# Layer-1 experts in half tiles: two 64-token halves of one tile, each with its own expert and weights

## What is computed

```
scores = sigmoid(x @ gate_w.T)
topv, topi = top_k(scores, 2);  topv = topv / topv.sum()
dw[token, topi] += topv
y = shared_mlp(x)
for each expert e:                      # silu(x@w1.T) * (x@w3.T), then @ w2.T
    y += mlp_e(x) * dw[:, e]
```

## Time and profile before

| | us |
|---|---|
| median of 3 runs | 1307.13 |
| lowest and highest | 1302.79, 1315.53 |
| span of the profiled execution, first to last instruction (the page gives no other time for it) | 1301.1 |
| PE busy | 1046.2 |
| DVE busy | 912.1 |
| ACT busy | 491.2 |
| POOL busy | 466.3 |

### The profile page before, as it was taken

The page is one execution under the profiler, slowest core; times in us unless marked ns, Lnnn a source line. Parts: engine busy times, 40 slices in busy tenths (PEclk is TensorE's granted clock), DMA queues, the critical chain, the costliest instruction groups (busy, mean ns, idle before and its releaser), DMA issues.

```text
span 1301.1 us, 18688 instructions
## 1 busy us (share of the span) xinstructions
PE 1046.2 (80%) x6112; PEld 621.6 (48%) x6112; DVE 912.1 (70%) x1502; ACT 491.2 (38%) x1114; POOL 466.3 (36%) x333
## 2 busy tenths in 40 slices
PE   1989898777778788873777778998898979998785
PEld 1644555444444444441634444564455635554343
DVE  3186576889998989896547646666665566756686
ACT  2110035544554544551112134445543454435332
POOL 1000010688888888862180012333232313331000
PEclk9798899989998988895879798999898989989798
DMA  9900071689987888889530043544253525441121
GB/s 360 340 5 0 1 189 41 139 141 155 158 149 132 149 137 152 148 129 180 121 122 4 12 90 77 114 106 103 68 125 79 119 61 128 92 98 34 25 72 51
DMA packets 111187, 143.26 MB, mean 110 GB/s; under 512 B 30022, under 2 KB 97334, under 8 KB 110902
## 3 DMA queue, kind: packets, MB, share of 16 engines
q0 software_dynamic: 34464, 77.92, 33.4%
q1 hardware_dynamic: 76630, 64.14, 17.8%
HBM read 72.80 MB, written 39.46 MB: 86 GB/s over the span
## 4 chain that ended last, share of the span: by engine, by line
PE 28%; DMA 16%; DVE 10%; issue 6%; POOL 4%; ACT 4%; SPq 3%; ACTq 0%; DVEq 0%; POOLq 0%
DMA sum<-yo,to_i 11%; PE bank L1395 4%; PE bank L1402 3%; PE bank L1823 3%; PE bank L1862 3%; DMA crow<-cp_d 2%; PE bank L1806 2%; DVE cv L2051 2%; PE bank L1815 2%; POOL xg L1148 2%; POOL sum L1141 2%; PE bank L666 2%; PE bank L1848 1%; PE bank L678 1%; PE bank L1389 1%
## 5 line engine op out<-in xcount | busy, mean ns | idle before, releaser
L1468 POOL DMA_INDIRECT sum<-yo,to_i x48 | 76.4, 1592 | 319.9 <-ACT yo L1422 299.8
L1148 POOL DMA_INDIRECT xg<-xn_d,token_i x80 | 99.7, 1247 | 243.6 <-DVE to_i L441 160.4
L1141 POOL DMA_INDIRECT sum<-yo,to_i x80 | 160.8, 2010 | 45.5 <-issue 44.6
L988 PE MATMUL bank<-areaA,xgT 128*128 x320 | 130.8, 537 | 16.4 <-issue 12.8
L1005 PE MATMUL bank<-areaA,hidT 88*128 x320 | 92.7, 414 | 42.7 <-ACT hidT L1053 32.4
L1993 DVE TENSOR_TENSOR areaD<-areaD,gb 128x512 f32<-128x512 f32 x128 | 87.3, 687 | 24.2 <-ACT areaD L1949 23.2
L1949 ACT ACTIVATE areaD<-bank 128x512 f32<-128x512 f32 x128 | 75.9, 594 | 62.7 <-PE bank L1815 59.7
L1121 DVE TENSOR_TENSOR_SCAN xnT<-areaB,xnT 128x1024 f32<-128x1024 f32 x42 | 96.2, 2290 | 3.3
L1005 PEld LDWEIGHTS bank<-areaA,hidT 88*128 88x128 f32 x320 | 56.9, 197 | 76.0 <-issue 71.1
L988 PEld LDWEIGHTS bank<-areaA,xgT 128*128 128x128 f32 x320 | 61.1, 209 | 61.7 <-issue 46.6
L666 PE MATMUL bank<-xnT,areaB 128*128 128x512 f32 x192 | 89.2, 613 | 0.8 <-DVE y L696 0.8
(11 more groups left out here) (327 smaller groups left out, 2210.3 us busy)
## 6 DMA issues: line engine op xcount, KB each, us to landing
y<-xnT POOLq DMA_DIRECT2D x21, 1024.0 KB, 8.9
wst<-gu_f SPq DMA_DIRECT2D x96, 176.0 KB
y<-areaB POOLq DMA_DIRECT2D x11, 1024.0 KB, 8.6
wst<-down_f SPq DMA_DIRECT2D x48, 176.0 KB
gu_f<-in_gu POOLq DMA_DIRECT2D x1, 5632.0 KB, 19.8
areaA<-in_gu SPq DMA_DIRECT2D x2, 2816.0 KB
sum<-yo SPq DMA_DIRECT2D x2, 2176.0 KB, 18.0
down_f<-in_down POOLq DMA_DIRECT2D x1, 2816.0 KB, 25.9
```

Source lines behind the costliest of these rows:

```text
L988: last = nc.tensor.matmul(bank[:, GB + q % 2, 0:2 * FI], xgT[:, q % 2, k, :], wgu0_of(e, k), start=(k == 0), stop=(k == KD - 1))
L1141: nc.gpsimd.indirect_dma_start(sum0_d[q % 2], bass.IndirectOffsetOnAxis(ap=to_i[:, q:q + 1], axis=0), yo[:, q % 5, :], None, compute_op=AL ...
L1148: nc.gpsimd.indirect_dma_start(xg[:, q % 5, :], None, xn_d[0], bass.IndirectOffsetOnAxis(ap=token_i[:, q:q + 1], axis=0)).then_inc(s.gathe ...
L1468: nc.gpsimd.indirect_dma_start(sum1_d, bass.IndirectOffsetOnAxis(ap=to_i[:, q:q + 1], axis=0), yo[:, q % 4, :], None, compute_op=ALU.add). ...
```

## The change

Layer 1's tiles keep 128 rows, but each is now two units of 64 rows with an expert of its own. Experts are padded to multiples of 64, so that 40 tiles (80 units) hold the worst case. `UNITS = (1, 2)` says so for the two layers; the two spare columns (`AHEAD`) of the routing tables fall away in both. For each half, gate, up and down use that half's weights: every product of 128 token columns becomes two of 64 columns, which write partitions 0 to 63 and 64 to 127 of the same bank. SP reads two expert numbers and loads two sets of weights per tile, one transfer for each expert's gate and up and one for its down. Gate and up get two slots (`wgu1`), reloaded after the gate and up product of tile q-2; down gets three (`wd1`), reloaded as before. ACT reads two expert numbers and copies the routing weights in two halves. Functions that nothing called (`route_tensor`, `route_vector`, `shared_tensor`, `shared_scalar`, `shared_vector`) are deleted, so line numbers fall by up to 180.

```diff
-def tiles_of(k):
-    n = (T * k + E * (P - 1)) // P
+HALF = P // 2
+UNITS = (1, 2)
+def tiles_of(k, units):
+    rows = P // units
+    n = -(-((T * k + E * (rows - 1)) // rows) // units)
     return n + n % 2
...
-        vec.done(nc.vector.tensor_tensor(m["cmp"], incl[:, :, TT - 1:TT].to_broadcast([P, E, E]),
-                                         iota128[:, None, :].to_broadcast([P, E, E]), ALU.is_gt))
+        vec.done(nc.vector.tensor_tensor(m["cmp"], incl[:, :, TT - 1:TT].to_broadcast([P, E, E * UNITS[l]]),
+                                         iota64[:, None, ::2 // UNITS[l]].to_broadcast([P, E, E * UNITS[l]]), ALU.is_gt))
...
+        NU = (NT0, NT1)[l] * UNITS[l]
+        vec.done(nc.vector.tensor_tensor(m["q_cmp"], m["tile_end"].unsqueeze(1).to_broadcast([P, NU, E]),
+                                         iota[:, 0:NU, None].to_broadcast([P, NU, E]), ALU.is_le))
...
+    HALVES = [slice(i * HALF, (i + 1) * HALF) for i in range(2)]
+    def experts_of(eng, q):
+        return [eng.value_load(expert_i[0:1, 2 * q + i:2 * q + i + 1], min_val=0, max_val=E - 1) for i in range(2)]
...
             if part == 2 and 1 <= q <= NT1:
                 eb = EB + (q - 1) % 2
+                pe.wait_ge(wd_in[(q - 1) % WR], 32 * ((q - 1) // WR + 1))
                 pe.wait_ge(q1.hT_ready, q)
                 for h in range(2):
-                    last = nc.tensor.matmul(bank[:, eb, 0:D], hidT[:, (q - 1) % 2, h, :], wd_of(q - 1, h), start=(h == 0), stop=(h == 1))
+                    for i, r in enumerate(HALVES):
+                        last = nc.tensor.matmul(bank[r, eb, 0:D], hidT[:, (q - 1) % 2, h, r], wd_of(q - 1, i, h), start=(h == 0), stop=(h == 1))
                 last.then_inc(q1.y_full, 1)
             if part == 2 and q < NT1:
                 eb = EB + q % 2
-                pe.wait_ge(w_in_slot[q % WR], 16 * (3 * (q // WR) + 3))
+                pe.wait_ge(wgu_in[q % WG], 32 * (q // WG + 1))
                 pe.wait_ge(q1.xT_ready, q + 1)
                 for k in range(KD):
-                    last = nc.tensor.matmul(bank[:, eb, 0:2 * FI], xgT[:, q % 2, k, :], wgu_of(q, k), start=(k == 0), stop=(k == KD - 1))
+                    for i, r in enumerate(HALVES):
+                        last = nc.tensor.matmul(bank[r, eb, 0:2 * FI], xgT[:, q % 2, k, r], wgu_of(q, i, k), start=(k == 0), stop=(k == KD - 1))
                 last.then_inc(q1.gu_full, 1)
...
-                e = act.value_load(expert_i[0:1, q:q + 1], min_val=0, max_val=E - 1)
+                e = experts_of(act, q)
                 act.wait_ge(q1.xT_full, q + 1)
-                nc.scalar.activation(slot_w[:, q % 4:q % 4 + 1], xg[:, q % 4, bass.ds(D + e, 1)], ACT.Copy)
+                for i, r in enumerate(HALVES):
+                    nc.scalar.activation(slot_w[r, q % 4:q % 4 + 1], xg[r, q % 4, bass.ds(D + e[i], 1)], ACT.Copy)
...
-                e = sp.value_load(expert_i[0:1, q:q + 1], min_val=0, max_val=E - 1)
+                e = experts_of(sp, q)
+                if q >= WG:
+                    sp.wait_ge(q1.gu_full, q - WG + 1)
+                for i in range(2):
+                    sp.dma_start(wgu1[:, q % WG, i, :].rearrange("p (k f) -> p k f", k=KD),
+                                 gu1_f[bass.ds(e[i], 1), :, :].rearrange("e (k p) f -> p (e k) f", k=KD)).then_inc(wgu_in[q % WG], 16)
                 if q >= WR:
                     sp.wait_ge(q1.y_full, q - WR + 1)
-                for k in range(KD):
-                    sp.dma_start(wgu_of(q, k), gu1_f[bass.ds(e, 1), k * P:(k + 1) * P, :].rearrange("e p f -> (e p) f")).then_inc(w_in_slot[q % WR], 16)
-                sp.dma_start(wst[0:FH, q % WR, KD * 2 * FI:].rearrange("p (h d) -> p h d", h=2),
-                             down1_f[bass.ds(e, 1), :, :].rearrange("e (h f) d -> f (e h) d", h=2)).then_inc(w_in_slot[q % WR], 16)
+                for i in range(2):
+                    sp.dma_start(wd1[:, q % WR, i, :].rearrange("p (h d) -> p h d", h=2),
+                                 down1_f[bass.ds(e[i], 1), :, :].rearrange("e (h f) d -> f (e h) d", h=2)).then_inc(wd_in[q % WR], 16)
```

More of the change, by code:

```diff
@@ L243, in combine_store @@
         sp.dma_start(xn_d[l].rearrange("(t p) d -> p t d", p=P)[:, :, D:], m["combine"]).then_inc(ly[l].xn_stored, 16)
-    def route_tensor(pe, l, K, wr, nr, m):
-        s = ly[l]
-        NT = (NT0, NT1)[l] + AHEAD
-        pe.wait_ge(s.tr_free, KD * TT // 4)
-        pe.wait_ge(s.w_router, 16 * (2 - l))
-        for t in range(TT):
-            for k in range(KD):
-                last = nc.tensor.matmul(bank[:, 4, t * nr:(t + 1) * nr], xnT[:, k, t * P:(t + 1) * P], wr[:, k, :],
-                                        start=(k == 0), stop=(k == KD - 1))
-        last.then_inc(s.logits, 1)
-        pe.wait_ge(s.mask_ready, l + 1)
-        nc.tensor.matmul(bank[:, 5, 0:TT * E], before[:, :], m["mask"], start=True, stop=True).then_inc(s.ranks, 1)
-        nc.tensor.matmul(bank[:, 6, 0:TT * E], ones[:, :], m["mask"], start=True, stop=True).then_inc(s.ranks, 1)
-        pe.wait_ge(s.onehots, l + 1)
-        for n in range(TT * K):
-            last = nc.tensor.matmul(bank[:, 7, 0:NT], m["row_1h"][:, n, :], m["tile_1h"][:, n, :],
-                                    start=(n == 0), stop=(n == TT * K - 1))
-        last.then_inc(s.tokens, 1)
     def side_bank(pe, free, n):
@@ L291, in route_tokens_tensor @@
         s = ly[l]
[L292 removed]
+        NT = (NT0, NT1)[l]
         pe.wait_ge(s.onehots, l + 1)
@@ L543, in route_memory @@
+        nc.vector.scalar_tensor_tensor(to_i[:, 0:NT], m["q_sum"][:, 0:NT], -1.0, bank[:, 6, 0:NT], ALU.add, ALU.add).then_inc(s.indices, 1)
     def route_memory(scr, l, K, nr):
-        NT = (NT0, NT1)[l] + AHEAD
+        NT = (NT0, NT1)[l]
         at = [0]
@@ L606, in shared_scalar @@
-    def shared_scalar(act, l, F, th, beside=None):
-        s = ly[l]
-        def block(c):
-            for f in range(F):
-                act.wait_ge(s.sh_in, c * F + f + 1)
-                act.wait_ge(s.sh_free, c * F + f + 1)
-                nc.scalar.activation(th[:, f % 2, :], bank[:, 2 * (f % 2), :], ACT.Tanh, scale=0.5).then_inc(s.sh_tanh, 1)
-        if beside is None:
-            with act.Fori(0, NB) as c:
-                block(c)
-        else:
-            for c in range(NB):
-                block(c)
-                beside(c)
@@ L1217, in _program @@
     PAIRS = CH // 2
-    WF, WR = KD * 2 * FI + 2 * D, 3
+    WG, WR = 2, 3
     with ExitStack() as c1a, ExitStack() as c1:
@@ L1309, in _program @@
         ring_free = [sem(f"ring_free{k}") for k in range(2)]
-        w_in_slot = [sem(f"w_in_slot{k}") for k in range(WR)]
+        wgu_in = [sem(f"wgu_in{k}") for k in range(WG)]
+        wd_in = [sem(f"wd_in{k}") for k in range(WR)]
         ST, XT, CS, YB, EB = 2, 5, 3, 4, 6
```

194 lines of the change are left out of this document (22 added, 172 removed).

## The result

| | before | after |
|---|---|---|
| median, us | 1308.27 (1302.79 to 1315.53, 4 runs) | 1363.11 (1354.73 to 1366.43, 4 runs) |
| profiled span, us | 1301.1 | 1360.9 |
| mean granted clock of the span | 0.908 | 0.879 |

The change is slower: 1.037 of the time before, 95% interval 1.033 to 1.041. The two medians of the table stand 54.8 us (4.2%) apart, so the loss is 48 to 55 us. I had forecast 1312 with a range up to 1332, so the result lies outside, behind even rival B's 1341.

The account below looks back on a forecast made before the run. PE was taken to set the pace in steps with experts, ACT and DVE in projections. Span 1301.1 - 22.0 + 2.4 + 18.2 + 4 + 2 + 1 = 1306.7, plus 6.0 gives 1312.7, stated as 1312 us; range 1289 to 1332.

Parts of the forecast that it names:

- rival B: SP's queue: pieces back up behind doubled weights, 4 us instead of 2.1 on 11 chunks, more half clock: 1341 us; chance 0.26.
- +18.2 us forecast: SP's queue: total cost of small pieces arriving later behind the weights, over 11 chunks near weights and 4 others.
- +4 forecast: PE's clock: one or two more half-clock stretches after long waits, less one in the part without experts; bounds 0 to 10.
- 2.1 us per chunk: SP's queue: delay of pieces that follow weights: moved wait +1.0, four transfers for three +0.4, doubled bytes ahead +0.7.
- The slack: Chunks' pieces: of 11 near weights, six had no slack, three a little (1.4 us each), two enough; four others 0.3 each.
- the upper bound of 32: SP's queue: top of the 11 to 32 us range for late pieces, by the bounds of issue and queue.
- -22.0: Batches 2 and 3: saving from eight tiles fewer: steps 8.4, to step 8's transposes 4.9, convolutions 4.5, gates 4.2 us.
- covered in the steps: ACT: an extra copy and number read, some 0.5 us per tile, hidden by idle time in steps; +2 overall, bounds 0 to 7.
- I forecast 8.7: Projections of batch 3: saving without experts, from convolutions 4.5 us and gates 4.2 us.
- rival C: PE: the halves run one after the other instead of side by side, adding 90 us: 1403 us; chance 0.02.
- my 0 to 6: PE: bounds on the halves' cost from one more grouping change per tile; taken as 0.06 us a tile, 2.4 us.
- Over 40 us is B: Sign in PE's waits for pieces: about 27 us forecast, under 15 the faster rival (0.24), over 40 the slower queue-backup rival.

Follow-up runs that it names:

- e3: Kernel before, with SP's weights also waiting for the gate and up product of tile q-2; bytes, transfers and tiles unchanged: 1335.85 us, 1.0234.
- e8: Changed kernel, own transfer order, with 16 identity products on PE in front of each chunk's wait for its pieces while experts run: 1364.83 us, 1.0419.
- e13: Changed kernel, own transfer order, with 7 identity products on PE in front of each chunk's wait for its pieces: 1358.0 us, 1.0346.
- e9: Changed kernel, weights of a step's first three ticks behind the pieces, expert numbers and routing-weight copies on POOL instead of ACT: 1287.92 us, 0.9892.
- e11: Kernel before, small pieces ahead of the weights, its one expert number and copy on POOL instead of ACT: 1285.08 us, 0.9842.
- e10: Changed kernel in its own transfer order, expert numbers and routing-weight copies on POOL instead of ACT: 1360.4 us, 1.0443.
- e12: Kernel before, small pieces ahead of the weights, ACT reading the number twice and copying routing weights in two halves: 1298.12 us, 0.9966.
- e6: Changed kernel, weights of a step's first three ticks behind the pieces, ACT's number reads and routing copies behind its gathered rows' copy: 1308.52 us, 0.9975.
- e2: Kernel before, with SP issuing a chunk's small pieces ahead of the weights: 1287.82 us, 0.9874.
- e7: Kernel before, small pieces ahead of the weights, ACT's one number and copy moved behind the gathered rows' copy: 1297.38 us, 0.9882.

## Why the prediction was wrong

The direction of the mechanism was right and its size wrong; rival B came nearest, and I gave it 0.26. Two terms of the sum failed: the waits for the pieces (+18.2 us forecast, +31.5 measured) and, farther off, the clock that follows them (+4 forecast, +32.7 by PE's busy time).

**The step that failed: "2.1 us per chunk".** All three parts can be read at the chunk of the earlier trace rows. The weights were issued 0.94 us ahead of the state product before (817.12 and 818.06) and 0.34 behind it now (816.42 and 816.08): the moved wait is 1.28 us for my 1.0. From the weights' issue to the pieces' it takes 2.97 us for 1.43: +1.54 for my +0.4, of which 0.84 is one slow issue that the next chunk doesn't have. From there to the product it is 5.07 for 4.74: +0.33 for my +0.7, but at the next chunk it is 6.49. Together 3.15 us, and the wait grew by 3.20, where I had 2.1. The queue's part was too small for a reason that the old trace held: I took 4.02 us as the time with no weights ahead, but the last weights had been issued 1.9 us before. In batch 3, with no experts, a product started 3.44 us after its pieces' first issue without a wait that the profile lists (1235.59 and 1239.03), so one tile of weights already cost 1.3 us or more and not 0.7.

The slack failed as well. By the formula of the prediction, 9 chunks have weights in the same tick or the one before and 5 have them two ticks back, not 11 and 4. I gave them 1.2 us each in the mean (18.2 over 15; six times 2.1 is 12.6, not 12.8). In the trace PE waits for the pieces of every one of the 14, from 0.66 to 5.05 us each. Together that is 42.5 us for 8.5 before, 2.4 more for each. The five with weights two ticks back, of which I counted four at 0.3 us each, take 10.4 us of it, for 1.5 before. Their weights, issued later and for longer, now end 1.1 us or less ahead of the pieces, and these take 5.6 to 6.5 us from issue to product, where three that PE waited for before took 3.7 to 4.0. In all it is +31.5 us (42.8 against 11.3), at the upper bound of 32. e3 has the moved wait alone: 15.5 us more of waits, where my sum held it at 1.0 us a chunk and at most some 10 us, and 31 us of time.

**The clock: "+4, bounds 0 to 10".** By the busy time of batches 0 and 1 it was +32.7, some 3 of it the halves' own. I treated a stretch at 1.2 GHz as an accident after the longest wait; here one came behind 9 of 12 waits. Before the change the waits for pieces were 10 in all with one of 3.00 us, and I took the bound from how often a stretch followed those. e8 and e13 show that PE's products regain most of their length when PE is kept busy in the waits; by how much the time would fall with the clock alone restored is open.

**What went: "-22.0".** Right in the steps. On PE's timeline of batch 2, the places of the earlier trace rows:
```profile
1210.16 0.39 PE L1635 MATMUL bank<-crow,seg_l 94*128 94x512 bf16 x1
...
1231.98 1.07 PE L1699 MATMUL bank<-S,xC 128*64 128x512 f32 x2 [1.61 <-DVE S L1928]
1234.01 1.16 PE L1691 MATMUL bank<-ident,ys 128*128 128x128 f32 x8
```
21.8 and 2.0 us where I took 22.8 and 2.9 from the earlier trace rows: 15.3 saved for 13.3. In the projections of batch 3 I forecast 8.7 and the stretch fell by 2.2 (39.6 for 41.8). The wait for hidden values went and another took its place, on the same engine:
```profile
1251.52 3.75 PE L1626 MATMUL bank<-w_out,areaD 128*128 128x256 f32 x8 [7.45 <-DVE sq_sum L1837]
1255.06 0.42 PE L1627 MATMUL bank<-ones,sq_sum 128*128 128x2 f32 x2
```
The output product of batch 2 stands in PE's queue between two projections and waits 7.45 us for DVE's sum of squares; PE is at the 1.2 GHz level from 1246.8 to 1257.0, and the output product takes 3.54 us to the next start for 1.80 before (1190.27 to 1192.07). Here PE does not set the pace, and work taken from it turned into another wait, with a stretch at the lower clock. e9 (no experts in batch 3) and e11 (with them) show the same exchange in a stretch where neither has a late piece. Waits of PE from 1170 to 1300 us, e9:
```profile
PE bank L1639 <- DVE sq_sum L1850: 11.3, 4, 7.4
...
PE bank L1656 <- DVE areaD L1895: 4.6, 1, 4.6
```
and e11:
```profile
PE bank L1390 <- DVE hid L1436: 6.1, 1, 6.1
PE bank L1817 <- DVE sq_sum L2028: 5.5, 4, 2.1
```

**ACT: "covered in the steps".** False as a statement, without effect in the change (e10): it becomes some 10 to 12 us once the pieces are on time (e12, e9). In e6 the addition lay between two handovers to PE, which sets the pace, and there a half-idle engine did not cover it.

**What held.** The halves run side by side; rival C is out. The change of grouping costs about what I took, 0.06 us a tile. The earlier trace rows can't show this, as the state product behind gate and up works on 64 columns too. A tile with the full-width seg product behind it shows it, after:
```profile
1166.94 1.08 PE L1209 MATMUL bank<-wd,hidT 88*64 88x256 f32 x8
1167.86 1.35 PE L1217 MATMUL bank<-wgu,xgT 128*64 128x352 f32 x8
1169.15 0.39 PE L1635 MATMUL bank<-crow,seg_l 94*128 94x512 bf16 x1
```
and before:
```profile
825.84 1.13 PE L1395 MATMUL bank<-wst,hidT 88*128 88x256 f32 x4
826.81 1.35 PE L1402 MATMUL bank<-wst,xgT 128*128 128x352 f32 x4
828.00 0.38 PE L1815 MATMUL bank<-crow,seg_l 94*128 94x512 bf16 x1
```
That is 2.21 us for 2.16. A whole batch gives more. Batch 0 of e9 (halves) and then of e2 (full tiles), both at a granted clock of 0.97:
```profile
759.80:888.70 128.90, 116.84 (x1127) 63.05 (x1127) 84.06 (x163) 57.65 (x126) 43.69 (x56) 0.97 0.64 174
```
```profile
761.40:888.60 127.20, 115.17 (x1011) 67.33 (x1011) 83.92 (x163) 57.85 (x142) 36.56 (x28) 0.97 0.46 107
```
PE is busy 1.7 us more for 15 tiles, 0.11 a tile, which makes an estimate of 4.4 us over 40 tiles, inside my 0 to 6. The Trainium skill (TensorEngine Tiling (Array Packing), Tiling Modes, Key Properties) says that changing the tiling mode drains the engine. Gate and up, at whose end the grouping changes back, takes 1.29 us to the seg product for 1.19; the trace agrees in that there is a price, and can't tell whether a drain is what it pays for. The weights of gate and up came in time: L1217 has no idle time before it in the page, and their load into the array waited for them once, 0.8 us. "Over 40 us is B" was the sign that I had named, and 42.8 came.

## What to carry to other kernels

Before adding bytes or a later wait to a queue, list what else is issued behind it and who needs that next; small loads with a near deadline go first, bulk loads with slack behind them. Here the reordering was worth 1.3% in the kernel before and 3.3 points in the changed one. Price a moved wait by the round: where a queue waits for a product of the engine that in turn waits for the queue's loads, take the whole way from that product's end to the use of the load (8.2 to 9.6 us here) and set against it the work that the engine has left. The shortfall comes back in every round, also in those that had slack in the old trace. And price what follows a wait on TensorE: here the lower clock behind the waits weighed as much in PE's busy time as the waits in its idle time.

## What was not expected of the hardware

- 16 products of the identity in fp32 (32 instructions of 128 columns) took 3.73 us, 0.117 each. They brought the granted clock of batches 0 and 1 back to 0.96 and 0.93, from 0.89 and 0.85: PE had work where it had waited before.
- The issue of two down transfers took 1.75 us at 817.59 and 0.91 at 834.49: an issue in the same queue can stand for 0.8 us, in front of everything behind it.
- From the first issue of the pieces to their product: 5.07 us (819.39 to 824.46) and 6.49 (835.44 to 841.93) behind two sets of weights, against 4.74 right behind one, 4.02 where one had been issued 1.9 us before, and 3.44 in batch 3 with no weights about; the pieces are the same each time.
- On ACT, reading two expert numbers shows as 0.95 us in which the engine does nothing else (e6, 986.76), more than the 0.41 of the two copies that use them. Over all tiles of the scan it is 0.66 us a tile; one number at the same place takes 0.18 (e7).
